# First layer of a graph network: seven buffers for the equal-edge comparisons, and source numbers spread over the partitions by TensorE

## The chip, the cores and the metric

The kernel runs on one core of a Trainium2 chip. A core has five engines with a queue of instructions each: TensorE (PE; its weight loads are listed as PEld), VectorE (DVE), ScalarE (ACT), GpSimd (POOL) and SyncE (SP), which here only issues DMAs. They meet through semaphores. The metric is the device time of one execution in microseconds.

## The reference, cut to what matters

A network of four graph layers with residual and layer norm; 6250 nodes of 256 features, 100000 edges sorted by destination. The change touches the first layer's sum over edges and what is computed beside it:

```python
gathered = edge_val[:, None] * x[edge_col]                    # edge_row = src, edge_col = dst
support = jax.ops.segment_sum(gathered, edge_row, num_segments=N)
out = jax.nn.relu(jnp.concatenate([x, support], axis=1) @ W + b)
x = layernorm(x + out)
```

So each edge takes the row of `x` at its destination, times its weight, and adds it to the row of its source in `support`. Destinations are sorted, sources are not. The later layers sum by destination (attention, and two of normalised or plain sums).

## The kernel before

`scatter_by_source` (L1546) is the stage of the first layer. The edges stand in 784 tiles of 128 (`P`); a loop of 49 turns handles 16 tiles (`RING`) each, in two halves of 8 (`HALF`). Every engine runs its own written-out loop over the same turns; what orders them are the semaphores, there is no scheduler. In a tile:

- DVE makes two 128x128 matrices (L1823, L1825): `onehots`, which edge has which destination within a window of 128 nodes, and `same_source`, which edges of the tile have the same source, times their weights. For `same_source` it compares `source_row`, the tile's 128 source numbers along the free dimension, the same on all partitions, with `source_float`, the same numbers one per partition. There are four buffers of each (`BUFS`), so DVE can be four tiles ahead (`crossed`).
- PE multiplies them to `cross` (L1751), adds to the edge counts by destination (`counts_bank`, L1757), ACT copies `cross` to SBUF (L1709), PE multiplies it with the window of `x` (`rows_bank`, L1728), ACT copies the result to `rows` (L1686), and POOL adds the 128 rows to `support` in HBM with an indirect DMA (L1606). Equal sources of one tile all carry the full sum, so all but one of them must go to spare rows.
- That is what `index_half` (L1776) works out on DVE, eight tiles at once: it compares `source_row` with `source_float` again, masked by `earlier` (`scrap`, L1781), and puts the row numbers of the next half into `index` (L1795). It comes after the eight tiles of a half, and before DVE adds the half's counts to `histogram` (L1835). The read of a window's base into a register stands at each half's head.

`source_row` is loaded by SP (L1659), one broadcast DMA from HBM to 128 partitions per half (512 KB), in int32. SP waits before it until `same_source` of the half that stood there is done.

Beside it, in this first pass, the stage adds up values of equal edges. Seven times a turn (`NEAR`), before every second tile from tile 2 to tile 14, DVE compares `tail_row`, seven tiles of keys on all partitions, with `tail_key` (`compare`, L1807); the result goes into one of two buffers `same_edge`, and PE multiplies it with `near_values` into `totals` (`add_same`, L1739), matmuls with two columns, 15 a turn. Before it overwrites a buffer DVE waits until PE has used it (`same_used`). `tail_row` is loaded once a turn by SP (L1637), first in the turn's list, as soon as the seventh comparison of the turn before is done. SP's list of a turn is: `tail_row`, then for each half the window of `x`, zeros for `matrix`, `source_row`, zeros again.

A matmul of float32 operands is two instructions here, each with its weight load.

## Time and profile before

| | us |
|---|---|
| median of 3 runs | 7642.86 |
| lowest, highest | 7641.15, 7646.06 |
| the profiled execution, its own time | 7624.4 |
| its span in the profile | 7622.7 |
| the stage's turns in it | 114.8 to 1995.4 |

The profile is of one execution. A group of instructions is named by the engine, the line and the tiles, written<-read. "Busy" is time in which the engine executes, "idle before" the time in front of an instruction with what ended it in brackets. The granted clock is TensorE's: 1.0 is 2.4 GHz, 0.5 is 1.2 GHz. PE is busy for 80% of the whole span, POOL for 67%, DVE for 44%, ACT for 19%. A turn of the stage's loop shows in the timeline as the same pattern every 38 us or so.

### The profile page before, as it was taken

To read this page: it belongs to the slowest core of one execution; us is meant where nothing else is said; L and a number is where in the kernel's file an instruction comes from. 1 tells how busy PE (TensorE), PEld (TensorE's weight loads), DVE (VectorE), ACT (ScalarE), POOL (GpSimd) and SP (SyncE) were. 2 spreads that over 40 slices of the span, in tenths; PEclk is the share of its full clock that TensorE was granted. 3 is DMA by queue.
4 is the path that set the end of the run, shared out by engine and by line. 5 is a ranking of instruction groups with operands and counts; after the bars stand their busy time and mean duration, and the time that the engine had idled before them with its cause. 6 is when DMAs were issued, how large, how long until landed. Compare 5 with 4: busy or idle time off the path is not lost. (4 is left out here: it accounts for less than half of the span.)

```text
span 7622.7 us, 120614 instructions
## 1 busy us (share of the span) xinstructions
PE 6092.7 (80%) x30188; PEld 4294.4 (56%) x30188; DVE 3383.4 (44%) x13118; ACT 1434.8 (19%) x5010; POOL 5078.8 (67%) x4839
## 2 busy tenths in 40 slices
PE   3777777777673788886777777999799989998997
PEld 2445454444562565555666665666566656665655
DVE  3444444444353666664555553444333323333444
ACT  1222222222221122221222221111101000010001
POOL 3666666666674677775777775666577767776775
PEclk9777777777686999996555558999899999999998
DMA  7877777777532444442333337888599979988996
GB/s 261 192 176 146 153 156 155 155 156 155 114 105 82 112 116 117 116 117 73 82 80 82 83 83 236 287 283 286 190 318 312 309 256 319 308 265 297 305 308 214
DMA packets 752803, 1440.90 MB, mean 189 GB/s; under 512 B 155688, under 2 KB 483292, under 8 KB 749956
## 3 DMA queue, kind: packets, MB, share of 16 engines
q1 hardware_dynamic: 460276, 886.96, 34.2%
q0 software_dynamic: 289936, 523.75, 30.7%
q10 hardware_dynamic: 2304, 26.74, 0.8%
q8 instruction: 134, 2.20, 0.1%
q14 instruction: 153, 1.25, 0.1%
HBM read 1140.97 MB, written 295.98 MB: 189 GB/s over the span
## 5 line engine op out<-in xcount | busy, mean ns | idle before, releaser
L736 POOL DMA_INDIRECT rows<-gcn_rows,index x1632 | 1551.0, 950 | 658.0 <-issue 456.5
L1277 POOL DMA_INDIRECT rows<-gat_rows,index x1568 | 1500.3, 957 | 640.8 <-issue 463.7
L1606 POOL DMA_INDIRECT support<-rows,index x784 | 1211.9, 1546 | 691.9 <-ACT rows L1686 399.5
L832 PEld LDWEIGHTS bank<-onehots,rows 128*128 128x128 f32 x8704 | 1143.7, 193 | 607.9 <-issue 547.0
L832 PE MATMUL bank<-onehots,rows 128*128 128x128 f32 x8704 | 1181.3, 278 | 159.2 <-DMA rows<-gcn_rows,index 77.6
L1408 PE MATMUL bank<-onehots,rows 128*128 128x128 f32 (+1 forms) x4704 | 946.9, 338 | 328.5 <-DVE rows L1484 328.0
L1408 PEld LDWEIGHTS bank<-onehots,rows 128*128 128x128 f32 (+1 forms) x4704 | 720.6, 202 | 530.0 <-issue 323.0
L844 PE MATMUL dense_bank<-matrix,edge_space 128*128 128x512 f32 x1792 | 892.7, 619 | 0.0
L1751 PE MATMUL cross_bank<-same_source,onehots 128*128 128x128 f32 x1568 | 428.9, 363 | 569.8 <-DVE same_source L1825 569.8
L736 POOL DMA_INDIRECT rows<-norm,index x544 | 516.5, 949 | 286.3 <-issue 152.0
L1751 PEld LDWEIGHTS cross_bank<-same_source,onehots 128*128 128x128 f32 x1568 | 334.3, 243 | 661.1 <-issue 534.8
L844 PE MATMUL dense_bank<-alpha,edge_space 128*128 128x512 f32 x1344 | 670.3, 620 | 12.7 <-DVE acc L899 12.7
L1728 PE MATMUL rows_bank<-x_window,cross 128*128 128x256 f32 x1568 | 659.2, 514 | 0.0
L881 DVE TENSOR_SCALAR onehots<-iota,half_offset,edge_values 128x128 f32<-128x128 f32 x2176 | 589.3, 363 | 26.7 <-issue 8.1
L844 PEld LDWEIGHTS dense_bank<-matrix,edge_space 128*128 128x128 f32 x1792 | 310.7, 193 | 240.4 <-issue 239.1
L1781 DVE SCALAR_TENSOR_TENSOR scrap<-source_row,edge_space,earlier 128x128 f32<-128x128 int32 x792 | 224.6, 348 | 440.1 <-DMA source_row<-in_src_flat 440.1
L1728 PEld LDWEIGHTS rows_bank<-x_window,cross 128*128 128x128 f32 x1568 | 284.1, 227 | 220.6 <-issue 214.4
L1709 ACT COPY cross<-cross_bank 128x128 f32<-128x128 f32 x784 | 208.6, 266 | 967.9 <-PE counts_bank L1757 967.4
L1686 ACT COPY rows<-rows_bank 128x256 f32<-128x256 f32 x784 | 292.1, 373 | 401.6 <-PE rows_bank L1728 398.7
L1479 DVE TENSOR_SCALAR onehots<-iota,half_offset 128x128 f32<-128x128 f32 x1568 | 361.9, 302 | 8.8
L1757 PE MATMUL counts_bank<-onehots,values 128*3 128x128 f32 x1568 | 359.9, 319 | 0.0
L844 PEld LDWEIGHTS dense_bank<-alpha,edge_space 128*128 128x128 f32 x1344 | 234.1, 193 | 196.0 <-issue 194.5
(305 smaller groups left out, 7253.4 us busy)
## 6 DMA issues: line engine op xcount, KB each, us to landing
matrix<-matrix SPq DMA_DIRECT2D x448, 512.0 KB, 4.0
alpha<-matrix SPq DMA_DIRECT2D x336, 512.0 KB
matrix<-zeros SPq DMA_DIRECT2D x196, 512.0 KB, 8.0
edge_space<-gcn_rows SPq DMA_DIRECT2D x588, 128.0 KB, 5.2
dst_row<-in_dst_flat SPq DMA_DIRECT2D x100, 512.0 KB
source_row<-in_src_flat SPq DMA_DIRECT2D x99, 512.0 KB, 7.5
support<-zeros ACTq DMA_DIRECT2D x16, 1632.0 KB, 28.0
rows<-gcn_rows,index POOLq DMA_INDIRECT x1632, 5.2
```

The source lines that it names most:

```text
L736: nc.gpsimd.indirect_dma_start(rows[:, k, :], None, table, bass.IndirectOffsetOnAxis(ap=index[:, k:k + 1], axis=0),).then_inc(gathered[k], 16)
L832: done = nc.tensor.matmul(by_chunk(banks[h])[:, c, :], rows[:, k, c * P:(c + 1) * P], onehots[:, k, :], start=first and c == 0, stop=final ...
L844: done = nc.tensor.matmul(dense_banks[c][:, 0:GROUP], table_rows[:, n, c * P:(c + 1) * P], matrix[n].rearrange("p (n v) -> p n v", v=2)[:, ...
L881: made = nc.vector.tensor_scalar(onehots[:, k, :], g.iota[:], g.half_offset[:, tile], weights[:, 0, tile], ALU.is_equal, ALU.mult)
L1277: nc.gpsimd.indirect_dma_start(rows[:, k, :], None, table, bass.IndirectOffsetOnAxis(ap=index[:, k:k + 1], axis=0),).then_inc(gathered[k], 16)
L1408: done = nc.tensor.matmul(to, left, onehots[:, k, :], start=first and c == 0, stop=final and c == chunks - 1)
L1479: made = nc.vector.tensor_scalar(onehots[:, k, :], g.iota[:], g.half_offset[:, bass.ds(i * RING + k, 1)], None, ALU.is_equal)
L1606: nc.gpsimd.indirect_dma_start(support[k % COPIES], bass.IndirectOffsetOnAxis(ap=index[:, k // HALF, k % HALF:k % HALF + 1], axis=0), rows ...
L1686: nc.scalar.copy(rows[:, k % HALF, :], rows_bank[k % 2][:, 0:g.features]).then_inc(s.rows_ready, 1)
L1728: nc.tensor.matmul(rows_bank[k % 2][:, 0:g.features], cross[:, k % BUFS, :], x_window[:, k // HALF, :], start=True, stop=True).then_inc(s. ...
L1751: nc.tensor.matmul(cross_bank[k % 2][:, 0:P], onehots[:, b, :], same_source[:, b, :], start=True, stop=True)
L1757: nc.tensor.matmul(counts_bank[k // HALF][0:3, 0:P], values[:, k // HALF, k % HALF, :], onehots[:, b, :], start=(k % HALF == 0), stop=(k % ...
```

## The change

`same_edge` gets seven buffers, one for each comparison of a turn; DVE waits for the use of the same buffer in the turn before, not for the use two comparisons ago. ACT's `keep_totals` waits for the same use by a number that fits the new start value.

`source_row` is no longer loaded. ACT copies the eight columns of `source_float` of the next half to `source_columns`. PE takes each of these columns, repeated to 128, as the stationary operand and the identity matrix as the moving one, which gives the column's 128 numbers along the free dimension on all partitions, in float32. Four of them fill one PSUM bank, `row_bank`; ACT copies it to `source_row`. A half needs two such batches, issued after tiles 2 and 4 of the half before, and ACT's copies stand before those of tiles 3 and 5. `index_half` waits for the second copy (`row_ready`). To free a PSUM bank the two halves' counts share one.

```diff
-        source_row = sbuf("source_row", [P, 2, HALF, P], INT32)
+        source_row = sbuf("source_row", [P, 2, HALF, P])
+        source_columns = sbuf("source_columns", [P, HALF])
...
-            same_edge = sbuf("same_edge", [P, 2, 3 * P])
+            same_edge = sbuf("same_edge", [P, NEAR, 3 * P])
...
-        counts_bank = [psum(f"counts_bank{n}") for n in range(2)]
+        counts = psum("counts_bank")
+        counts_bank = [counts[:, h * P:(h + 1) * P] for h in range(2)]
+        row_bank = psum("row_bank")
...
-                        sync.wait_ge(s.matrices, i * RING + HALF * (h + 1))
-                        sync.dma_start(
-                            source_row[:, h, :, :].rearrange("p k e -> p (k e)"),
-                            g.source_flat[0:1, bass.ds((i * 2 + h) * (HALF * P), HALF * P)]
-                            .to_broadcast([P, HALF * P])).then_inc(row_loaded[h], 16)
...
+                def copy_columns(half):
+
+                    if not isinstance(half, int):
+                        act.wait_ge(s.row_turned, half * 2)
+                    act.sem_inc(s.issued, 1)
+                    nc.scalar.copy(source_columns[:], g.source_float[:, bass.ds(half * HALF, HALF)]
+                                   ).then_inc(s.columns_ready, 1)
+
+                def copy_row(half, h, batch):
+
+                    act.wait_ge(s.row_turned, half * 2 + (batch + 1))
+                    if not isinstance(half, int) and batch == 0:
+                        act.wait_ge(s.matrices, half * HALF + (RING - HALF))
+                    act.sem_inc(s.issued, 1)
+                    nc.scalar.copy(source_row[:, h, batch * BATCH:(batch + 1) * BATCH, :].rearrange("p k e -> p (k e)"),
+                                   row_bank[:]).then_inc(s.row_ready, 1)
...
+                        if k % HALF == 1:
+                            copy_columns(i * 2 + (k // HALF + 1))
+                        if k % HALF == 3:
+                            copy_row(i * 2 + (k // HALF + 1), 1 - k // HALF, 0)
+                        if k % HALF == 5:
+                            copy_row(i * 2 + (k // HALF + 1), 1 - k // HALF, 1)
...
+                def source_rows(half, batch):
+
+                    if batch == 0:
+                        pe.wait_ge(s.columns_ready, half + 1)
+                    if batch or not isinstance(half, int):
+                        pe.wait_ge(s.row_ready, half * 2 + batch)
+                    for n in range(BATCH):
+                        column = source_columns[:, batch * BATCH + n:batch * BATCH + n + 1].to_broadcast([P, P])
+                        done = nc.tensor.matmul(row_bank[:, n * P:(n + 1) * P], column, g.identity[:], start=True,
+                                                stop=True)
+                    done.then_inc(s.row_turned, 1)
...
+                        if k % HALF in (2, 4):
+                            source_rows(i * 2 + (k // HALF + 1), k % HALF // 2 - 1)
...
-                    dve.wait_ge(row_loaded[h], i * 16 + 16 * (ahead + 1))
+                    dve.wait_ge(s.row_ready, i * 4 + (2 * (2 * ahead + h) + 2))
...
-                    dve.wait_ge(s.same_used, i * NEAR + max(2, r + 1))
+                    dve.wait_ge(s.same_used, i * NEAR + (r + 1))
...
-                    nc.vector.tensor_scalar(same_edge[:, r % 2, 0:(high - low + 1) * P], tail_row[:, low * P:(high + 1) * P],
+                    nc.vector.tensor_scalar(same_edge[:, r, 0:(high - low + 1) * P], tail_row[:, low * P:(high + 1) * P],
```

On PE, tile 2 of a turn before the change (the names are tiles, written<-moving operand, stationary operand; REGISTER_ALU works out a semaphore's value):

```order
L1751 MATMUL cross_bank_418<-same_source,onehots 128x128
L1757 MATMUL counts_bank_422<-onehots,values 3x128
L1725 REGISTER_ALU
L1728 MATMUL rows_bank_421<-x_window,cross 128x256
L1734 ISA
L1739 MATMUL totals<-near_values,same_edge 128x2
L1748 REGISTER_ALU
L1751 MATMUL cross_bank_419<-same_source,onehots 128x128
```

And after it:

```order
L1784 MATMUL cross_bank_419<-same_source,onehots 128x128
L1790 MATMUL counts_bank<-onehots,values 3x128
L1744 REGISTER_ALU
L1747 MATMUL rows_bank_422<-x_window,cross 128x256
L1753 ISA
L1758 MATMUL totals<-near_values,same_edge 128x2
L1765 REGISTER_ALU
L1767 REGISTER_ALU
L1770 MATMUL row_bank<-identity,source_columns 128x128 x4
L1781 REGISTER_ALU
L1784 MATMUL cross_bank_420<-same_source,onehots 128x128
```

The four source matmuls stand between the tile's `totals` and the next tile's `cross`; tile 4 and the second half have the same.

On ACT, between the copies of tiles 2 and 3 before the change (`rows` of tile 1, then `cross` of tile 3):

```order
L1683 REGISTER_ALU
L1686 COPY rows<-rows_bank_421 128x256
L1708 REGISTER_ALU
L1709 COPY cross<-cross_bank_419 128x128
```

And after it:

```order
L1676 REGISTER_ALU
L1679 COPY rows<-rows_bank_422 128x256
L1703 REGISTER_ALU
L1705 REGISTER_ALU
L1707 COPY source_row<-row_bank 128x512
L1727 REGISTER_ALU
L1728 COPY cross<-cross_bank_420 128x128
```

The copy of the source rows, with its wait, now stands ahead of the copy of `cross`.

On SP, the start of a turn's list before the change:

```order
L1637 DMA tail_row<-key_row 128x896
L1651 TENSOR_LOAD half_base
L1651 ISA x2
L1655 ISA
L1655 DMA x_window<-in_x 128x256
L1645 DMA matrix<-zeros 128x1024
L1659 DMA source_row<-in_src_flat 128x1024
L1645 DMA matrix<-zeros 128x1024
```

And after it:

```order
L1640 DMA tail_row<-key_row 128x896
L1654 TENSOR_LOAD half_base
L1654 ISA x2
L1658 ISA
L1658 DMA x_window<-in_x 128x256
L1648 DMA matrix<-zeros 128x1024 x2
```

The source load and the wait before it are gone, the two loads of zeros stand together.

## Rows read from the trace of the kernel before

**Rows 1.** Who waited for whom, 104 to 2004 us: total us, times, longest.
```profile
PE cross_bank L1751 <- DVE same_source L1825: 569.8, 98, 82.2
...
DVE scrap L1781 <- DMA source_row<-in_src_flat: 440.1, 49, 12.9
...
DVE same_edge L1807 <- PE totals L1739: 349.9, 147, 3.9
...
POOL support L1606 <- issue: 193.8, 516, 4.9
```

**Rows 2.** The instructions that write `cross_bank`: min/median/max ns, first and last start.
```profile
L1751 PE MATMUL cross_bank<-same_source,onehots x1568: 272/356/582, 114.8 to 1995.4; 128*128 128x128 f32 x196
```

**Rows 3.** Busy time by stretch: length, PE, PEld, DVE, ACT, POOL, granted clock, DMA.
```profile
500.00:1900.00 1400.00, 1033.89 (x4581) 685.93 (x4580) 577.09 (x2798) 390.87 (x1308) 895.49 (x580) 0.75 0.73 154
...
1020.00:1029.50 9.50, 9.50 (x32) 6.34 (x33) 2.93 (x11) 2.25 (x8) 6.16 (x4) 0.50 0.65 96
...
1035.00:1042.00 7.00, 0.00 (x0) 0.00 (x0) 3.48 (x22) 0.78 (x4) 4.60 (x3) 0.64 1.10 286
...
1042.00:1047.00 5.00, 4.82 (x15) 2.69 (x16) 2.76 (x13) 1.04 (x4) 0.02 (x1) 0.50 0.59 137
```

**Rows 4.** Timeline of DVE at a turn's middle and end: start, length, what, [idle before].
```profile
1016.18 0.28 DVE L1835 TENSOR_TENSOR histogram<-histogram,counts_bank 3x128 f32 x1 [2.13 <-PE counts_bank L1757]
...
1026.30 0.29 DVE L1807 TENSOR_SCALAR same_edge<-tail_row,tail_key 128x128 f32<-128x128 f32 x1 [3.89 <-PE totals L1739]
...
1036.00 0.35 DVE L1781 SCALAR_TENSOR_TENSOR scrap<-source_row,edge_space,earlier 128x128 f32<-128x128 int32 x1 [8.13 <-DMA source_row<-in_src_flat]
...
1039.07 0.17 DVE L1795 TENSOR_TENSOR index<-moved,edge_space 128x8 int32<-128x8 f32 x1 [0.48 <-DMA support<-rows,index]
...
1039.30 0.28 DVE L1835 TENSOR_TENSOR histogram<-histogram,counts_bank 3x128 f32 x1
```

**Rows 5.** Timeline of SP at the same turn's end.
```profile
1026.75 0.33 SPq L1637 DMA_DIRECT2D tail_row<-key_row  x1
...
1029.08 0.33 SPq L1659 DMA_DIRECT2D source_row<-in_src_flat  x1
```

**Rows 6.** Timeline of PE in the same turn and at its end.
```profile
1010.65 0.38 PE L1751 MATMUL cross_bank<-same_source,onehots 128*128 128x128 f32 x2
...
1011.82 0.50 PE L1739 MATMUL totals<-near_values,same_edge 128*128 128x2 f32 x4
...
1018.32 0.49 PE L1751 MATMUL cross_bank<-same_source,onehots 128*128 128x128 f32 x2 [1.74 <-DVE same_source L1825]
...
1021.13 0.59 PE L1757 MATMUL counts_bank<-onehots,values 128*3 128x128 f32 x2
...
1023.23 0.59 PE L1757 MATMUL counts_bank<-onehots,values 128*3 128x128 f32 x2
...
1042.18 0.79 PE L1751 MATMUL cross_bank<-same_source,onehots 128*128 128x128 f32 x2 [7.23 <-DVE same_source L1825]
```

**Rows 7.** PE in a later stage, timeline and granted clock of a stretch.
```profile
4635.96 2.04 PE L832 MATMUL bank<-onehots,rows 128*128 128x128 f32 x8 [19.25 <-DMA rows<-norm,index]
...
4637.80 3.62 PE L844 MATMUL dense_bank<-alpha,edge_space 128*128 128x512 f32 x4
...
4644.48 1.05 PE L832 MATMUL bank<-onehots,rows 128*128 128x128 f32 x8
...
4645.36 1.97 PE L844 MATMUL dense_bank<-alpha,edge_space 128*128 128x512 f32 x4
...
4636.00:4637.00 1.00, 1.00 (x5) 1.00 (x6) 1.00 (x6) 0.00 (x0) 0.69 (x2) 0.50 1.05 385
```

**Rows 8.** Groups of the page: count, busy us, mean ns, idle before by releaser.
```profile
L1606 POOL DMA_INDIRECT support<-rows,index x784 | 1211.9, 1546 | 691.9 <-ACT rows L1686 399.5
...
L1686 ACT COPY rows<-rows_bank 128x256 f32<-128x256 f32 x784 | 292.1, 373 | 401.6 <-PE rows_bank L1728 398.7
```

More of the change, by code:

```diff
@@ L1576, in scatter_by_source @@
         rows_bank = [psum(f"rows_bank{n}") for n in range(2)]
-        counts_bank = [psum(f"counts_bank{n}") for n in range(2)]
+        counts = psum("counts_bank")
+        counts_bank = [counts[:, h * P:(h + 1) * P] for h in range(2)]
+        row_bank = psum("row_bank")
         names = [f"scattered{k}" for k in range(HALF)]
-        with phase(nc, "kept", "x_loaded0", "x_loaded1", "row_loaded0", "row_loaded1", "own", "index_ready",
+        with phase(nc, "kept", "x_loaded0", "x_loaded1", "columns_ready", "row_turned", "row_ready", "own", "index_ready",
                    "issued", "matrices", "crossed", "cross_copied", "multiplied", "rows_ready", "counted",
@@ L1582, in scatter_by_source @@
             scattered = s[-HALF:]
-            x_loaded, row_loaded = [s.x_loaded0, s.x_loaded1], [s.row_loaded0, s.row_loaded1]
+            x_loaded = [s.x_loaded0, s.x_loaded1]
             @block.gpsimd
@@ L1671, in _ @@
                     sync.wait_ge(s.kept, 16 * len(later))
-                sync.wait_ge(s.matrices, g.tiles + HALF)
-                sync.dma_start(source_row[:, 0, :, :].rearrange("p k e -> p (k e)"),
-                               g.source_flat[0:1, 0:HALF * P].to_broadcast([P, HALF * P])
-                               ).then_inc(row_loaded[0], 16)
             @block.scalar
@@ L1693, in keep_totals @@
                 def keep_totals(i):
-                    act.wait_ge(s.same_used, i * NEAR + (NEAR + 2))
+                    act.wait_ge(s.same_used, i * NEAR + 2 * NEAR)
                     act.sem_inc(s.issued, 1)
@@ L1698, in keep_totals @@
                                    ).then_inc(s.near_ready, 1)
+                def copy_columns(half):
[11 more added lines that the diff above has]
+                                   row_bank[:]).then_inc(s.row_ready, 1)
                 if first_pass:
                     copy_near(0)
+                copy_columns(0)
+                for batch in range(2):
+                    copy_row(0, 0, batch)
                 with act.Fori(0, g.tiles // RING) as i:
                     for k in range(RING):
+                        if k % HALF == 1:
[4 more added lines that the diff above has]
+                            copy_row(i * 2 + (k // HALF + 1), 1 - k // HALF, 1)
                         if k % HALF == 0:
@@ L1738, in add_same @@
                     for w in range(low, high + 1):
-                        done = nc.tensor.matmul(totals[:, w - 1, :], same_edge[:, r % 2, (w - low) * P:(w - low + 1) * P],
+                        done = nc.tensor.matmul(totals[:, w - 1, :], same_edge[:, r, (w - low) * P:(w - low + 1) * P],
                                                 near_values[:, r, :], start=r == 0, stop=r == NEAR - 1)
                     done.then_inc(s.same_used, 1)
+                def source_rows(half, batch):
[8 more added lines that the diff above has]
+                    done.then_inc(s.row_turned, 1)
                 if first_pass:
-                    pe.sem_inc(s.same_used, 2)
+                    pe.sem_inc(s.same_used, NEAR)
+                for batch in range(2):
+                    source_rows(0, batch)
                 with pe.Fori(0, g.tiles // RING) as i:
```

## The prediction

> **What bounds the kernel now.** I read the list of who waited for whom first, for the first layer's stage. TensorE (PE) waits 98 times for `same_source` of VectorE (DVE), twice in each of the 49 turns; without the one long wait of 82.2 us at the start that is 487.6 us, or 9.95 us a turn. DVE waits 49 times, 440.1 us, for the DMA of `source_row`, and 147 times, 349.9 us, for PE's `totals` [rows 1]. The turns fill the time between the first and last `cross` matmul, 114.8 to 1995.4 us, so one turn takes 38.4 us [rows 2]. Inside the stage the granted clock is 0.75 on average, so PE stands at its lower level (1.2 GHz) for half of a turn, 19.2 us [rows 3].
>
> The timeline shows how a turn ends. DVE gets to its last comparison of equal edges, `same_edge` for r = 6, at 1026.30, after 3.89 us of waiting for `totals`, since two buffers are all it has. Only then may SyncE (SP) start `tail_row`, and the `source_row` load of the next turn's first half stands behind that in its queue: it starts at 1029.08 and lands for DVE's `scrap` at 1036.00, where DVE sat idle for 8.13 us. Comparisons, `index` and `histogram` follow, and PE gets its next `same_source` at 1042.18, after 7.23 us of idleness [rows 4 to 6]. So the late broadcast sets the turn, not its bandwidth. GpSimd (POOL) is no bound: 16 scatters of 1.55 us with 0.38 us between them (193.8 us / 516) are 30.8 us of 38.4, and most of its idle time is for ACT's `rows` [rows 1, 8].
>
> **Part by part, for one turn.** I split the turn into PE's work at full clock, its pauses, and what the low clock adds.
>
> A tile (cross, counts, rows) takes 1.17 us at full clock (1010.65 to 1011.82) and 2.10 us at the lower level (1021.13 to 1023.23) [rows 6]. So of each busy microsecond at the low level 1 - 1.17/2.10 = 0.44 is loss. Of the 7.0 us from 1035 to 1042, at 0.64 in the mean, 5.0 us were low while PE was idle [rows 3]; for the average pause at a turn's end of 8.2 us (9.95 less the 1.74 in the middle [rows 6]) I take 6.0. Low and busy are then 19.2 - 6.0 = 13.2 us, a loss of 5.8. Full-clock work is 38.4 - 9.95 - 5.8 = 22.6 us.
>
> *The pause at the turn's end.* With source rows out of PE and ACT, DVE needs no DMA there, and what is late next is the count of the half's last tile: `histogram` must come before the next half's matrices. In the middle of a turn this already is so, and it costs 1.74 us [rows 6]. There the way from `histogram` to PE's next matmul is 2.14 us (1016.18 to 1018.32), at the end it is 2.88 (1039.30 to 1042.18), for the register loads at the loop's head [rows 4, 6]; PE meanwhile has one more rows matmul to do (half a tile by its columns, 0.5). The end pause becomes 1.74 + 0.74 - 0.5 = 2.0 us, I take 2.1. That removes 6.1 us.
>
> *The source matmuls.* 16 a turn, four in a row, at tiles 2 and 4 of each half. Each is float32, 128x128 by 128x128, so two instructions. The nearest rows are runs of eight such instructions: 0.88 us at full clock (4644.48 to 4645.36), 1.84 us at the lower (4635.96 to 4637.80, granted clock 0.50) [rows 7]. Four runs are 3.5 us, and with 0.1 for each wait on a semaphore 4.0 us. From above, if each costs a quarter of a tile (which has four times 128 columns to move, `rows` counting twice), it is 16 x 0.29 + 0.4 = 5.1. They lie on PE's path, nothing hides them. None of the rows has a stationary operand that is one column repeated; I take it to cost what another does. A bound below nothing has no reason here.
>
> *ACT.* Four copies of 128x512 a turn and two of 128x8. A 128x256 copy is 0.37 us [rows 8], so 0.6 (at most 0.75) each: 2.6 us. ACT waits in order, so a copy that waits for `row_turned` holds back the copy of the next `cross`; but the four matmuls end before PE does the next cross and counts (0.6 us), which cover it. Nothing.
>
> *DVE's new wait.* `index_half` now waits for the second copy of source rows. After tile 3 is counted PE has half a tile, tile 4, a few `totals`, and two waits' worth of source matmuls (one run) to do, 3.1 us; copy 0.6; from the first `scrap` to `histogram` 3.30 (1036.00 to 1039.30) [rows 4]: 7.0 us. PE counts tile 7 after 3.1 + 1.2 + 1.2 + 0.5 + 0.6 = 6.6 us. At full clock DVE is later than before by 0.2 to 0.4, at the lower clock not at all. I put 0.2 a turn; bounds 0 and 2 (one per half).
>
> *Seven buffers.* DVE no longer waits for `totals` (7.1 us a turn), but it is then held by `crossed`, four tiles ahead of PE. Their use is that the last comparison, and so `tail_row` behind it, comes earlier: tile 9 is counted at 1021.7 (1021.13 and half a microsecond), so r = 6 could be done at 1022.5 in place of 1026.30, 3.8 us earlier [rows 4, 6]. By themselves they would thus take most of the pause away already. With the broadcast gone they only guard `tail_row` (448 KB by its size, against 512 KB of `source_row`, which took 6.9 us, 1029.08 to 1036.00 [rows 4, 5]): between comparison 6 and comparison 0 of the next turn PE does at least five tiles, a pause and two source runs, about 10 us.
>
> *DMA.* SP loses two loads and their waits per turn, 1 MB that landed in SBUF. Nobody waits for the others; nothing.
>
> *The low clock.* Now 13.2 us busy in it. In the turn shown it is there again at 1020, 1.7 us after PE resumes from the middle pause, and lasts at least the 9.5 us to 1029.5 while PE is wholly busy; after the end pause it lasts about 5 us more (1042 to 1047 at 0.50) [rows 3]. So a pause of 1.74 us is enough to lose the clock, and I expect two falls a turn as before. How it comes back: with the denser work of rows 7 it was back within 5.3 us of 19 us of idleness (4635.96 low, the run at 4644.48 full). The source matmuls are work of that density, and `totals`, with two columns each, are the opposite. I take 5 us per pause, 10 in all, a loss of 4.4. Bounds: 5 and 20.
>
> **Sum.** Work 22.6 + 4.0, pauses 2.1 + 1.7 + 0.2, low clock 4.4: 35.0 us a turn, 3.4 less than 38.4. Over 49 turns 167 us, and some 3 us since the first half needs no load (of 12.9 us that DVE waits for it [rows 1], the tail and x loads keep most). The profiled execution, 7624.4 us with a span of 7622.7, would become about 7454. It lies 18.5 us under the median of 7642.86; I take the same difference for the median: 7473 us. What comes after the stage begins when it ends, and its work is the same.
>
> **The rivals.** Each as 30.6 + 0.44 x L, L being low-clock busy time; 17.7 us of L would give all back.
>
> 1. *The clock pays for it (slower).* Place: the 10 us after each of the two pauses. If each costs what the middle one costs now, 10 us, then L = 20 and the turn is 39.4 us: +49 us, 7690. It decides from L = 17.7. For it: more work at low clock lasts longer, and the trace has that 10 us stretch with PE wholly busy. Against: rows 7. The Trainium skill ("TensorE: Matmul & The Clock Gate", Part 4, PE-mode transpose) says that transposes through the array do not count as activity for the clock gate. A matmul against the identity does a transpose's work; if that held for these ordinary matmuls too, this rival would be the likeliest and the sum 7690, else 7473. No row before the change settles it. Chance 0.12.
>
> 2. *The clock stays up.* The end pause is short enough to lose nothing: L = 5, 32.8 us a turn, 7366. Against it: the middle pause is shorter and loses it. Chance 0.08.
>
> 3. *A new wait eats it.* DVE's wait for `row_ready` costs 1 us per half and a source matmul costs 0.29: 35.0 + 1.8 + 1.1 = 37.9, 7616; either alone, 7525 to 7565. For it: the margin is 0.4 us. Against it: at low clock there is none. Chance 0.17 for over 7560.
>
> 4. *The broadcast isn't what ends the pause*, since x, tail or a scatter is late just behind it. `index` waits for landed scatters, and `tail_row` still starts late. A pause of 4 us in place of 2.1 gives 36.9 us a turn, 7566. For it: DMA is the slowest releaser here. Against it: five tiles lie between. Counted in 3.
>
> **How the numbers follow.** Forecast, 7390 to 7560: 0.63; rival 1 0.12, rival 2 0.08, rivals 3 and 4 0.17 together. Of rival 3 0.02 and of rival 1 0.01 lie within 0.2% of 7643 (15 us, about what a measurement of this kernel can tell from no change). Faster 0.63 + 0.08 + 0.15 = 0.86, same 0.03, slower 0.11. The range leaves out rival 1 and half of rival 2: 7390 to 7620.
>
> **What the profile after would show.** The stage ends near 1830 us; PE idle before `cross` some 4 us a turn, not 9.95; no wait of DVE for `totals` or for a source load; `row_bank` runs of 0.9 us at full clock; the mean granted clock in the stage over 0.8. A mean clock of 0.7 or less would speak for rival 1; runs of 1.2 us or a `scrap` that starts after the last count for rival 3. The forecast is wrong if PE's pauses stay long for another load, or if L is over 15 us.

## The result, and the profile after

The changed kernel takes 7559.15 us (median of 4 runs, 7555.93 to 7571.13), the kernel before 7642.0 (4 runs, 7631.09 to 7646.06). The ratio is 0.9903 with an interval of 0.989 to 0.9916: 83 us or 0.97% faster. A second series gave 0.9913 (0.9891 to 0.9935). The forecast was 7473 us, 170 us faster. So the direction held, and half the gain is missing.

The profiled executions have spans of 7554.4 and 7622.7 us, 68.3 apart. Where they differ is read from the instructions that write `cross_bank` after the change (min/median/max ns, first and last start):

```profile
L1784 PE MATMUL cross_bank<-same_source,onehots x1568: 272/275/583, 105.8 to 1934.0; 128*128 128x128 f32 x196
```

The new tile `row_bank`, in the same view:

```profile
L1770 PE MATMUL row_bank<-identity,source_columns x1584: 275/275/579, 90.4 to 1931.2; 128*128 128x128 f32 x198
L1707 ACT COPY source_row<-row_bank x198: 586/586/587, 92.6 to 1931.6; 128x512 f32<-128x512 f32 x198
```

Against 114.8 to 1995.4 before [rows 2] the stage starts 9.0 us earlier and its 49 turns are 52.4 us shorter, 1828.2 in place of 1880.6: 37.3 us a turn, not 38.4. That is 61.4 of the 68.3 us. The other 7 us lie in later stages, whose work is the same.

Who waited for whom, 104 to 2004 us (total us, times, longest):

```profile
DVE onehots L1858 <- PE counts_bank L1790: 546.4, 245, 4.5
...
DVE scrap L1816 <- ACT source_row L1707: 349.3, 98, 3.9
ACT source_row L1707 <- PE row_bank L1770: 283.7, 196, 2.8
...
PE cross_bank L1784 <- DVE same_source L1860: 207.1, 98, 10.5
...
DVE index L1830 <- DMA support<-rows,index: 43.8, 89, 0.5
```

These answer to [rows 1]. PE's 569.8 us of waiting for `same_source` are 207.1 now; without the one wait of 10.5 us at the start that is 4.0 us a turn, 9.95 before. DVE's waits for `totals` (349.9) and for the source load (440.1) are gone. Thus 5.9 us of idleness a turn went, but the turn is only 1.1 us shorter. The rest became work, and more of it under a lower clock. By stretch (length; busy time of PE, PEld, DVE, ACT, POOL; granted clock; DMA share and GB/s):

```profile
500.00:1900.00 1400.00, 1248.76 (x5893) 896.76 (x5891) 588.40 (x2872) 490.00 (x1570) 921.56 (x596) 0.77 0.69 132
1037.70:1041.10 3.40, 3.40 (x12) 2.08 (x12) 2.63 (x11) 1.24 (x5) 2.29 (x3) 0.56 1.09 278
1041.20:1051.30 10.10, 9.33 (x59) 6.91 (x58) 3.43 (x21) 4.65 (x14) 7.99 (x6) 0.99 0.60 67
1051.50:1065.00 13.50, 12.61 (x44) 9.35 (x45) 5.15 (x20) 2.86 (x9) 6.85 (x5) 0.51 0.64 154
1065.10:1075.20 10.10, 7.92 (x46) 5.43 (x46) 4.49 (x27) 4.32 (x15) 7.27 (x5) 0.99 0.65 116
```

The mean clock of the stage is 0.77, against 0.75 [rows 3]. PE is busy 89% of the time, not 74% (1248.76 and 1033.89 of 1400). One turn is four stretches: 3.4 us at the lower level (1.2 GHz, 0.50) after the pause at the turn's end, 10.2 us full, 13.7 us low from within the pause in the middle on, 10.2 us full. (The windows shown start up to 0.4 us beside the steps.) The steps of the granted clock in the trace lie at 1038.08, 1041.49, 1051.73 and 1065.39. PE's timeline over the same turn:

```profile
1036.74 0.48 PE L1784 MATMUL cross_bank<-same_source,onehots 128*128 128x128 f32 x2 [2.16 <-DVE same_source L1860]
...
1045.23 1.14 PE L1770 MATMUL row_bank<-identity,source_columns 128*128 128x128 f32 x8
1046.21 0.39 PE L1784 MATMUL cross_bank<-same_source,onehots 128*128 128x128 f32 x2
...
1052.39 0.79 PE L1784 MATMUL cross_bank<-same_source,onehots 128*128 128x128 f32 x2 [1.87 <-DVE same_source L1860]
...
1060.12 1.28 PE L1758 MATMUL totals<-near_values,same_edge 128*128 128x2 f32 x6
1061.26 2.05 PE L1770 MATMUL row_bank<-identity,source_columns 128*128 128x128 f32 x8
1063.10 0.64 PE L1784 MATMUL cross_bank<-same_source,onehots 128*128 128x128 f32 x2
...
1074.27 0.48 PE L1784 MATMUL cross_bank<-same_source,onehots 128*128 128x128 f32 x2 [2.18 <-DVE same_source L1860]
...
1089.91 0.79 PE L1784 MATMUL cross_bank<-same_source,onehots 128*128 128x128 f32 x2 [1.86 <-DVE same_source L1860]
```

Two things are to be seen. A run of four source matmuls takes 0.98 us at full clock (1045.23 to 1046.21) and 1.84 us at the lower (1061.26 to 1063.10); of the four runs of a settled turn three are at full clock and only this one is at the lower. And the next turn repeats this one: 1036.74 to 1074.27 and 1052.39 to 1089.91 are 37.5 us each, with the same pauses. By the distance between `histogram` instructions three early turns take 33.1, 34.8 and 37.7 us, and every one after them 37.4 to 37.7 us with halves of 21.6 and 15.9. Turns before the change vary between about 36 and 41 us.

### The profile page after: what moved, and what is told of

It is laid out like the page before. It is cut to its first block and busy times, and to the rows that moved or that the text cites. A ratio compares the mean times of both kernels' runs of the same rounds, so it can differ in the third digit from the quotient of the medians.

```text
span 7554.4 us, 124892 instructions
## 1 busy us (share of the span) xinstructions
PE 6340.0 (84%) x31772; PEld 4550.9 (60%) x31772; DVE 3376.6 (45%) x13118; ACT 1550.6 (21%) x5307; POOL 5078.6 (67%) x4839
## 3 DMA queue, kind: packets, MB, share of 16 engines
q0 software_dynamic: 289936, 523.75, 31.1%
## 5 line engine op out<-in xcount | busy, mean ns | idle before, releaser
L1747 PE MATMUL rows_bank<-x_window,cross 128*128 128x256 f32 x1568 | 683.8, 530 | 0.0
L1784 PE MATMUL cross_bank<-same_source,onehots 128*128 128x128 f32 x1568 | 399.3, 343 | 207.1 <-DVE same_source L1860 207.1
L1858 DVE TENSOR_SCALAR onehots<-iota,half_offset 128x128 f32<-128x128 f32 x784 | 248.8, 318 | 605.5 <-PE counts_bank L1790 546.4
L1816 DVE SCALAR_TENSOR_TENSOR scrap<-source_row,edge_space,earlier 128x128 f32<-128x128 f32 x792 | 224.4, 350 | 353.3 <-ACT source_row L1707 349.3
L1479 DVE TENSOR_SCALAR onehots<-iota,half_offset 128x128 f32<-128x128 f32 x1568 | 361.1, 301 | 8.2
```

Of the source, the lines that this page charges most:

```text
L1479: made = nc.vector.tensor_scalar(onehots[:, k, :], g.iota[:], g.half_offset[:, bass.ds(i * RING + k, 1)], None, ALU.is_equal)
L1747: nc.tensor.matmul(rows_bank[k % 2][:, 0:g.features], cross[:, k % BUFS, :], x_window[:, k // HALF, :], start=True, stop=True).then_inc(s. ...
L1784: nc.tensor.matmul(cross_bank[k % 2][:, 0:P], onehots[:, b, :], same_source[:, b, :], start=True, stop=True)
```

## The experiments

**How each turn is counted.** The forecast's own sum is used for every kernel: 22.6 us of full-clock work, the added matmuls, PE's idleness, and 0.44 for each busy microsecond at the lower level (L). Idleness and L are added up from PE's instructions and the steps of the granted clock, over the stage without its first and last turns; "turn" is the first to the last `cross` matmul over 49. The 22.6 was solved from the kernel before, so its row agrees by construction. In the others a turn is PE's busy and idle time in any case; what the agreement within 0.6 us tests is that the work without the matmuls stays 22.6 us and that 0.44 and the matmuls' price are right. The ratio is to the kernel before in the same series. PE's idleness is nearly all before `cross`, except in e4, e7, e8, e10 and e11, where 0.5 to 2.3 us of it stand elsewhere.

| kernel | ratio [interval] | added matmuls | idle | L | sum | turn, us |
|---|---|---|---|---|---|---|
| before | 1 | 0 | 10.1 | 13.5 | 38.6 | 38.4 |
| changed | 0.9903 [0.989, 0.9916] | 3.9 | 4.0 | 16.1 | 37.6 | 37.3 |
| e5, changed again | 0.9913 [0.9891, 0.9935] | 3.9 | 4.0 | 16.4 | 37.7 | 37.5 |
| e2, source matmuls only | 0.9933 [0.9911, 0.9956] | 3.9 | 4.0 | 16.4 | 37.7 | 37.4 |
| e1, seven buffers only | 0.9787 [0.975, 0.9824] | 0 | 6.2 | 14.2 | 35.0 | 34.9 |
| e12, the same again | 0.9741 [0.9722, 0.976] | 0 | 6.5 | 13.6 | 35.1 | 34.9 |
| e3, fill in the middle pause | 0.9618 [0.9575, 0.9662] | 3.9 + 1.6 | 2.7 | 3.5 | 32.3 | 31.8 |
| e9, fill in the end pause | 0.9703 [0.9676, 0.9731] | 3.9 + 1.6 | 2.5 | 8.7 | 34.4 | 34.1 |
| e6, fill before tile 14 | 0.9745 [0.9724, 0.9766] | 3.9 + 1.6 | 3.2 | 8.5 | 35.0 | 34.7 |
| e4, source matmuls in the pauses | 0.9597 [0.9562, 0.9633] | 3.9 | 3.4 | 4.2 | 31.7 | 31.1 |
| e11, the same again | 0.952 [0.9495, 0.9545] | 3.9 | 3.2 | 4.5 | 31.7 | 31.1 |
| e7, load before tail | 0.9693 [0.9671, 0.9715] | 0 | 5.5 | 13.1 | 33.9 | 33.8 |
| e10, e7 with seven buffers | 0.971 [0.9685, 0.9736] | 0 | 5.3 | 13.8 | 34.0 | 33.9 |
| e8, e7 with fill in both pauses | 0.9704 [0.9687, 0.9722] | 3.2 | 4.5 | 8.6 | 34.1 | 34.0 |

e1 to e4 ran in a series in which the other stages are slower (before takes 8994.7 us there; from the last `cross` matmul to the end e1 takes 7019 us and e12, the same kernel, 5618). This stage is as long as elsewhere: 34.9 us a turn in both e1 and e12, 31.1 in both e4 and e11. The ratios of that series are therefore nearer to 1 for the same saving, and the turn is what compares.

### e1 and e12: seven buffers alone

```diff
-            same_edge = sbuf("same_edge", [P, 2, 3 * P])
+            same_edge = sbuf("same_edge", [P, NEAR, 3 * P])
...
-                    pe.sem_inc(s.same_used, 2)
+                    pe.sem_inc(s.same_used, NEAR)
...
-                    dve.wait_ge(s.same_used, i * NEAR + max(2, r + 1))
+                    dve.wait_ge(s.same_used, i * NEAR + (r + 1))
```

ACT's wait in `keep_totals` changes along with them. The source load stays a DMA.

> The kernel before with seven buffers alone; the broadcast DMA of the source numbers stays. The clock theory (of the changed kernel's turn of 37.5 us, 16.3 us are busy work at the low clock, where 10 were forecast, and most of them follow the middle pause; pauses and matmul costs are as forecast): the last comparison of a turn ends 3.8 us earlier, the pause at the turn's end goes from some 8.4 to 4 to 5 us; with as much low clock as before a turn of 34.6 us (7455 us in all), with 16 us of low clock 36 us (7525). The rival theory (the added source matmuls, 4 us a turn on TensorE's path, take back what the shorter pause gives, and the clock only goes along): 34.6 us a turn, 7455, faster than the changed kernel by 100 us.

Measured: 8823.98 against 8994.7 us; turn 34.9 us. Since this is faster than the whole change, it was run again where the other stages run as in the first series.

> The kernel before with seven buffers alone, once more: its first run was on a chip on which all other stages were slower. By the balance it keeps its turn of 34.9 us on any chip, 3.5 us less than before, so the kernel before less 170 to 190 us, and faster than the whole change by some 100 us. If the first ratio (0.979) came from that chip's slower DMA, it comes out near the changed kernel's 0.990.

Measured: 7444.65 against 7636.9 us, 192 us less, interval 0.9722 to 0.976. Waits of e12 over its stage:

```profile
PE cross_bank L1751 <- DVE same_source L1825: 392.6, 98, 82.1
DVE scrap L1781 <- DMA source_row<-in_src_flat: 266.1, 55, 12.9
```

And a stretch of it (columns as above):

```profile
500.00:1600.00 1100.00, 896.92 (x3959) 596.40 (x3960) 500.91 (x2422) 337.21 (x1129) 780.87 (x504) 0.77 0.82 171
```

PE's wait for `same_source` falls from 569.8 to 392.6 us and DVE's for the source load from 440.1 to 266.1 [rows 1]: about 3.6 us a turn, all of it kept, since L hardly moves (13.5 and 13.6). The buffers alone give more than twice what the change gives.

### e2: the source matmuls alone

The changed kernel with the buffers put back (and with them PE's start value and ACT's wait):

```diff
-            same_edge = sbuf("same_edge", [P, NEAR, 3 * P])
+            same_edge = sbuf("same_edge", [P, 2, 3 * P])
...
-                    dve.wait_ge(s.same_used, i * NEAR + (r + 1))
+                    dve.wait_ge(s.same_used, i * NEAR + max(2, r + 1))
```

> The changed kernel with two buffers of same_edge in place of seven. Both theories: VectorE waits for totals again, but between the last comparison and the next tail_row lies time enough, so within 0.2% of the changed kernel's 7559 us. If the buffers carry a part of the gain it is slower by up to 3.8 us a turn, 7745.

Measured: 8940.8 us, ratio 0.9933; turn 37.4 us. Its waits:

```profile
DVE same_edge L1842 <- PE totals L1758: 385.6, 142, 3.9
PE cross_bank L1784 <- DVE same_source L1860: 206.6, 98, 10.4
```

And PE's timeline where it waited:

```profile
1005.53 0.48 PE L1784 MATMUL cross_bank<-same_source,onehots 128*128 128x128 f32 x2 [2.16 <-DVE same_source L1860]
...
1021.16 0.80 PE L1784 MATMUL cross_bank<-same_source,onehots 128*128 128x128 f32 x2 [1.85 <-DVE same_source L1860]
...
1043.01 0.48 PE L1784 MATMUL cross_bank<-same_source,onehots 128*128 128x128 f32 x2 [2.17 <-DVE same_source L1860]
```

DVE again waits 385.6 us for `totals`, and PE waits no longer than in the changed kernel, with the same two pauses and the same 37.5 us between turns. Once the source rows come from PE, the buffers hide nothing that anyone waits for. The parts overlap: each removes the same late load, the buffers for nothing, the matmuls for 3.9 us of PE's time and 2.9 us more at the lower clock.

### e3: seven unread matmuls in the middle pause

The changed kernel with matmuls that nobody reads, just ahead of PE's wait for tile 8:

```diff
+        idle_bank = psum("idle_bank")
...
+                        if k == HALF:
+                            for _ in range(7):
+                                nc.tensor.matmul(idle_bank[:, 0:P], g.identity[:], g.identity[:], start=True, stop=True)
                         pe.wait_ge(s.matrices, i * RING + (RING + k + 1))
```

> The changed kernel plus seven matmuls of the identity by itself, whose result nobody reads, in the pause in the middle of each turn (before TensorE's wait for tile 8's matrices): 1.6 us of added work in a pause of 1.9 us. Clock theory: the pause no longer costs the clock, the low stretch of 13.7 us that follows it in every turn goes, 0.44 x 13 = 5.7 us less a turn: 31.8 to 33 us a turn, 7280 to 7340 us in all. Rival theory: 37.5 us a turn or more, 7559 to 7600, whatever the clock does.

Measured: 8671.7 us, ratio 0.9618; turn 31.8 us. PE's timeline at e3's two pauses:

```profile
1013.13 0.48 PE L1788 MATMUL cross_bank<-same_source,onehots 128*128 128x128 f32 x2 [2.21 <-DVE same_source L1864]
...
1026.70 1.72 PE L1784 MATMUL idle_bank<-identity 128*128 128x128 f32 x14
1028.72 0.49 PE L1788 MATMUL cross_bank<-same_source,onehots 128*128 128x128 f32 x2 [0.30 <-DVE same_source L1864]
```

And its stretch:

```profile
500.00:1600.00 1100.00, 1013.87 (x6010) 749.19 (x6011) 565.43 (x2687) 453.60 (x1467) 869.66 (x561) 0.95 0.82 157
```

1.6 us of work without use shorten the turn by 5.5 us (269 us in all against e2 of the same series, whose turns are those of the changed kernel). The middle pause shrinks from 1.87 to 0.30 us, the mean clock goes from 0.77 to 0.95, and L from 16.1 to 3.5. This shows that the lower clock holds back the missing time, and how much it is: 0.44 x 12.6 = 5.5 us a turn.

The pause at the end, 2.2 us, is as long as before, and yet 12 of the 47 turns counted have no low clock at all. A stretch of 57.9 us at full clock with such a pause in it:

```profile
1048.30:1106.20 57.90, 53.04 (x334) 39.92 (x333) 29.33 (x141) 25.25 (x81) 46.38 (x30) 1.00 0.81 147
...
1076.51 0.48 PE L1788 MATMUL cross_bank<-same_source,onehots 128*128 128x128 f32 x2 [2.16 <-DVE same_source L1864]
```

So a pause of this length goes with a fall in every settled turn of the changed kernel and does not bring one by itself.

### e6 and e9: the same matmuls elsewhere

Is it the pause that costs the clock, or is there simply too little matmul work? e6 has the same seven at `if k == HALF + 6:`, where PE doesn't pause; e9 at `if k == 0:`, in the pause at the turn's end.

> The changed kernel plus the same seven matmuls of the identity once a turn, not in a pause but before tile 14, where TensorE has no pause of note. Clock theory: the work is the same as in the kernel that fills the middle pause, but the pause still costs the clock, so 0 to 1.6 us more a turn: 37.5 to 39.1 us a turn, the changed kernel plus 0 to 80 us. If the seven matmuls helped by their number alone, wherever they stand, it would be some 270 us faster than the changed kernel, as the kernel with the middle pause filled was.

> The changed kernel plus the seven unread matmuls of the identity in the pause at the turn's end alone (ahead of the wait for tile 0). In the changed kernel the low stretch after that pause is 3.4 us, the one after the middle pause 13.7 us. Clock theory: the short one goes, 1.5 us less a turn, and the long one stays: 36 us a turn, the kernel before less 140 to 170 us, so far less than with the middle pause filled (less 323 us). If any added dense work helps alike, less 300 us or more.

Measured: e6 7435.16 us against 7566.85 for the changed kernel (e5) in that series, 132 less, where none or a loss was expected. e9: 7402.63 against 7623.3 for before, 221 less where 140 to 170 was expected; turn 34.1 where 36 was. PE's timeline of e6, with the fill and both pauses:

```profile
1005.49 1.72 PE L1784 MATMUL idle_bank<-identity 128*128 128x128 f32 x14
...
1011.38 0.48 PE L1788 MATMUL cross_bank<-same_source,onehots 128*128 128x128 f32 x2 [1.18 <-DVE same_source L1864]
...
1025.73 0.49 PE L1788 MATMUL cross_bank<-same_source,onehots 128*128 128x128 f32 x2 [2.10 <-DVE same_source L1864]
```

Its stretch:

```profile
500.00:1600.00 1100.00, 997.80 (x5444) 733.07 (x5444) 499.29 (x2441) 411.01 (x1325) 788.55 (x508) 0.87 0.74 142
```

The fill and the end pause of e9:

```profile
1026.09 1.73 PE L1784 MATMUL idle_bank<-identity 128*128 128x128 f32 x14
1028.42 0.48 PE L1788 MATMUL cross_bank<-same_source,onehots 128*128 128x128 f32 x2 [0.61 <-DVE same_source L1864]
```

Its stretch:

```profile
500.00:1600.00 1100.00, 1021.35 (x5543) 756.45 (x5542) 502.82 (x2474) 420.10 (x1352) 803.25 (x518) 0.87 0.76 146
```

In both, one low stretch a turn is left (of 6.8 to 13.7 us in e6, of 6.8 or 10.2 in e9, once 3.4); it follows the middle pause, and L is 8.5 and 8.7. The theory "a filled pause saves what stood behind that pause" is too narrow: e9 fills the pause that has 3.4 us of low clock behind it, and the long stretch behind the other pause shrinks. e6 fills no pause; the one that follows is shorter (1.18, not 2.16 us): PE gets there later while DVE's matrices come when they came, so the matmuls may act in part as a fill of that pause. What stands: matmuls at any of three places shorten the turn by 2.6 to 5.5 us, the middle pause being the best of them.

### e4 and e11: the source matmuls in the pauses

If the pauses are there anyway, the work that the change adds can stand in them: both batches ahead of the wait of tiles 0 and 8, into two PSUM banks, with the column copies moved up.

```diff
-        row_bank = psum("row_bank")
+        row_bank = [psum(f"row_bank{n}") for n in range(2)]
...
-                        if k % HALF == 1:
-                            copy_columns(i * 2 + (k // HALF + 1))
-                        if k % HALF == 3:
+                        if k % HALF == 6:
+                            copy_columns(i * 2 + (k // HALF + 2))
+                        if k % HALF == 0:
                             copy_row(i * 2 + (k // HALF + 1), 1 - k // HALF, 0)
-                        if k % HALF == 5:
                             copy_row(i * 2 + (k // HALF + 1), 1 - k // HALF, 1)
...
+                        if k % HALF == 0:
+                            for batch in range(2):
+                                source_rows(i * 2 + (k // HALF + 1), batch)
                         pe.wait_ge(s.matrices, i * RING + (RING + k + 1))
...
-                        if k % HALF in (2, 4):
-                            source_rows(i * 2 + (k // HALF + 1), k % HALF // 2 - 1)
```

> The changed kernel with both batches of source matmuls (eight in a row, two PSUM banks) moved to the head of each half, before TensorE waits for the next half's matrices, so into its two pauses of about 2 us; the copies on ScalarE move along, and the columns are copied half a turn earlier. Clock theory: 3.6 us leave the path and both pauses are filled, so the clock falls less often: 26.8 us + 0.44 x 5 = 29 us, then GpSimd's 30.8 us of scatters is the bound: 31 us a turn, 7240 to 7300 in all. Rival theory: 37.5 - 3.6 = 33.9 us a turn, 7380.

> The kernel with the source matmuls in the pauses once more, beside the others of this call on one chip: a turn of 31.1 us as in its first run, the kernel before less 340 to 370 us, and faster than the reordered kernels by over 60 us.

Measured: e4 8635.94 us, ratio 0.9597; e11 **7259.11 us** (7254.89 to 7261.07) against 7623.3, ratio 0.952, interval 0.9495 to 0.9545. That is 364 us below the kernel before and 144 below e10 of the same series. Waits of e11 over its stage:

```profile
DVE index L1831 <- DMA support<-rows,index: 298.0, 86, 7.6
POOL support L1609 <- DMA support<-rows,index: 185.1, 396, 5.3
```

PE's timeline at the end of a pause with source matmuls in it:

```profile
1013.08 2.05 PE L1770 MATMUL row_bank<-identity,source_columns 128*128 128x128 f32 x16
1018.67 0.64 PE L1787 MATMUL cross_bank<-same_source,onehots 128*128 128x128 f32 x2 [3.54 <-DVE same_source L1861]
```

And its stretch:

```profile
500.00:1600.00 1100.00, 990.94 (x5629) 717.10 (x5629) 565.57 (x2734) 466.56 (x1493) 888.06 (x573) 0.93 0.82 160
```

The pauses did not both fill: the middle one is gone in 43 of 48 turns, the one at the end stands in 41 and is 2.3 us in the mean, behind the source matmuls. The same sixteen matmuls a turn cost 3.9 us as before, but the clock is 0.93 and L 4.5, nearly all of it behind the end pause. The turn is 31.1 us, and now DVE's `index` and POOL wait for scatters to land, 298.0 and 185.1 us. 16 scatters with what lies between them are 30.8 us by [rows 1, 8], so little more is to be had in front of POOL.

### e7, e8 and e10: the late load without any matmul

The load was late because SP issues `tail_row` first and that waits for the last comparison. So the kernel before, with `tail(i)` after the loads of the first half:

```diff
                 def loads(i):
-                    tail(i)
                     for h in range(2):
+                        if h == 1:
+                            tail(i)
```

> The kernel before (two buffers, broadcast DMA, no source matmuls) with one change in SyncE's list: tail_row is issued after the loads of a turn's first half and not ahead of them, so that the late load of source_row no longer stands behind the wait for the last comparison. Clock theory: the source numbers are there in time, the pauses are 4 us a turn as in the changed kernel, without its 4 us of source matmuls: 22.6 + 4.0 + 0.44 x (13 to 16) = 32.3 to 33.7 us a turn, the kernel before less 230 to 300 us. If the DMA itself were the bound (its bandwidth, or the scatters beside it), the turn would stay over 36 us.

> The same with seven unread matmuls of the identity at the head of each half, ahead of TensorE's wait for matrices. Clock theory: both pauses are filled, the clock stays up most of the time: 22.6 + 4.0 + 0.44 x 2 = 27.5 us, under GpSimd's 30.8 us of scatters, which then is the bound: 31 us a turn, the kernel before less 360 us or more. If the filled pauses give nothing, it is as the kernel with the reordered load alone, or up to 80 us slower.

> The kernel before with the reordered load and seven buffers, no source matmuls. What binds there by the balance 22.6 + pauses + 0.44 x low clock: VectorE no longer waits for totals (336.8 us in the reordered kernel), which were not on TensorE's path; so pauses of 4 to 5.5 us a turn and 33 to 34 us a turn, as the reordered kernel alone, the kernel before less 230 to 280 us.

Measured: e7 7395.44 us against 7633.26, ratio 0.9693 (238 us less, within the 230 to 300 expected) with a turn of 33.8 and 5.5 us of idleness where 4.0 were expected. e8, with e3's seven matmuls in both pauses (`if k % HALF == 0:`), 7403.71, ratio 0.9704, far from the 360 us expected. e10, e7 with seven buffers, 7403.68 against 7623.3, 220 less where 230 to 280 was expected; its ratio of 0.971 can't be told from e7's by the intervals. Waits of e7 over its stage:

```profile
DVE index L1796 <- DMA support<-rows,index: 280.6, 96, 9.1
...
DVE scrap L1782 <- DMA source_row<-in_src_flat: 63.7, 48, 2.9
```

And of e8:

```profile
DVE index L1800 <- DMA support<-rows,index: 374.2, 96, 12.1
ACT rows L1688 <- DMA support<-rows,index: 307.0, 206, 9.1
POOL support L1607 <- DMA support<-rows,index: 256.9, 371, 8.2
```

One line moved in SP's list takes DVE's wait for the load from 440.1 to 63.7 us [rows 1] and gives nearly three times the change's gain. The buffers add nothing to it: both cure the same thing. What is late next is the landing of the scatters, beside the 1 MB of source loads that still run. In e8 L falls from 13.1 to 8.6, worth 2.0 us, and idleness by 1.0, but 3.2 us of matmuls came in. `index` waits for scatters 94 us more than in e7, and ACT's `rows`, 116.4 us in e7, waits 307.0; PE then waits for ACT too, 107.8 us in place of 25.7:

```profile
PE rows_bank L1730 <- ACT cross L1711: 107.8, 99, 7.2
```

By these waits the matmuls bought clock that the scatters ate. In e11 the loads are gone, DVE waits 298.0 us and ACT's `rows` 111.5 in a turn that is 2.9 us shorter. This would be the one use of doing without the DMA; no run varies the DMA load by itself, so that step is argued from the two kernels' waits and not shown.

### e5: the changed kernel again

> The changed kernel itself, beside the kernels of this call on one chip. Both theories: its stage of the first layer takes the same 1828 us from first to last cross matmul as in the profile of the changed kernel (turn 37.3 us), and it is 60 to 90 us faster than the kernel before, whatever the other stages take on this chip.

Measured: 7566.85 against 7633.26 us, ratio 0.9913; stage 105.4 to 1943.0 us, turns of 37.5 us. The result came again.

## Why the prediction was half right

*The late load ends the turn.* Right: e7 changes only its place in the queue and gets 238 us.

*The pauses, 4.0 us a turn in place of 9.95.* Right: 207.1 us less 10.5 over 49 turns is 4.0; single pauses are 2.16 at the end (predicted 2.1) and 1.87 in the middle (1.74 and a part of the 0.2 of delay).

*The source matmuls, 4.0 us a turn.* Right. Runs of 0.98 and 1.84 us stand where the nearest rows had 0.88 and 1.84 [rows 7]; four at full clock are 3.9. The higher bound, a quarter of a tile each, was not needed, and a stationary operand of one repeated column costs what another does.

*ACT.* Right: 0.586 us a copy, 0.6 taken.

*DVE's new wait.* Right in size. In the middle of a turn `histogram` now starts straight behind `index`, where before it had waited 2.13 us for PE's count [rows 4]:

```profile
1050.30 0.17 DVE L1830 TENSOR_TENSOR index<-moved,edge_space 128x8 int32<-128x8 f32 x1 [0.50 <-DMA support<-rows,index]
1050.53 0.28 DVE L1870 TENSOR_TENSOR histogram<-histogram,counts_bank 3x128 f32 x1
```

PE's middle pause grew by 0.13 us against the one turn that the prediction read, and by 0.35 in the mean of the stage (1.54 to 1.89). So rival 3 had its mechanism, at a tenth to a third of its price. Rival 4, another load late, did not come: `index` waits at most 0.5 us for scatters.

*The start.* 9.0 us earlier, 3 predicted: tail and x loads held less of the first wait than assumed.

*Seven buffers.* The text said that the last comparison would come 3.8 us earlier and that this alone "would thus take most of the pause away already". It took 3.6 us, under half of the 8.2 at the turn's end. But the sum was never made for this part alone: 38.4 - 3.8 = 34.6 us a turn was there to be read, below the 35.0 forecast for the whole. e12 measured 34.9. The gain was credited to the pair, and the matmuls' own share, by the forecast's own terms, was below nothing. Measured, the matmuls make e12's 7444.65 into about 7559, some 110 us slower (in different series, whose times for before differ by 0.1%).

*The low clock.* This is the step that failed: "I take 5 us per pause, 10 in all, a loss of 4.4." Measured are 3.4 and 13.7 us, less about 0.7 in which PE was idle: L = 16.4 in each such turn, a loss of 7.2 us. That is 2.8 us a turn more than taken, 137 us over 49 turns, and covers the whole 113 us by which the stage missed its 35.0 us a turn (37.3 measured; the sum from measured parts gives 37.6). The term was bounded by 5 and 20, and the value was taken from the neighbour that suited: rows 7 say how fast the clock comes back in dense work after 19 us of idleness (by the clock's own step 5.5 us, where the text has 5.3). The prediction's own 13.2 us for the kernel before already said more: kept as it was, it gives 36.4 us a turn. No row gave a reason for it to fall to 10. The row of this stage, 9.5 us low with PE wholly busy after the middle pause [rows 3], said about 10 for that pause alone. It was called rival 1 and given 0.12, and what came is that rival stopped short of its break-even of 17.7. With 5 for the end and 10 for the middle the sum would have been 15 x 0.44 = 6.6 and 37.2 us a turn. That this comes so near is partly luck: the row was one turn with a long stretch, and in the mean of the stage before, 7.5 us of L stand behind the middle pause and 6.0 behind the end. After the change it is 12.8 and 3.3: the whole growth is behind the middle pause.

*The range and the signs.* The measured 7559 lies in the stated range of 7390 to 7620 and just within the forecast's 7390 to 7560, but with L at 16.1 and not 10, so the range did not hold it for its reason. The sign that it named for being wrong came: L is over 15 us. The mean clock is 0.77, not over 0.8, and the stage ends at 1934 us, not near 1830. Rival 2, the clock staying up, did not come.

*Rival 1's other ground.* The source matmuls do not fail to hold the clock. e3 puts seven plain matmuls against the identity into a pause and the mean clock goes from 0.77 to 0.95; e11 does it with the source matmuls themselves, 0.93. The Trainium skill ("TensorE: Matmul & The Clock Gate", Part 4) says of transposes in the array's transpose mode that they do not count as busy time in the same way; if that were read as a rule for an ordinary float32 matmul against the identity, these runs would speak against it. No run here has a transpose of that mode, so what it says of those stays open. What mattered was where the matmuls stand: behind tiles 2 and 4 of each half, three of the four runs come when the clock is up and one in the middle of the low stretch; ahead of tiles 0 and 8 the clock falls less often, L 4.5 in place of 16.1.

*What stays open.* Why the turns of the changed kernel (and of e2 and e5) settle into identical ones of 37.5 us, with one low stretch of 13.7 us in each, across two groups of six `totals`. Both small changes of a turn (e6, e9) ended this pattern, and in e3 a pause of 2.2 us often brings no fall, so part of the 16.4 us may belong to it and not to the pauses' lengths. A run that shifts the turn's length a little and leaves PE's work as it is could tell; none was made.

## What to carry to other kernels

When two edits attack one wait, make the sum for each alone and then for the pair: the second often pays its full price for a wait that the first removed, and one line's place in a DMA queue may do what both do. Where TensorE sits at its lower clock for half a stage, price added matmuls by where they stand: with sixteen of them in the pauses the turn took 31.1 us here, with the same sixteen between tiles 37.3 us. For the low clock take the rows of the same stage, and of two neighbours the one that speaks against the change when the break-even (17.7) lies near the bound.

## What the runs showed of the hardware

- Seven unread 128x128 float32 matmuls, 1.6 us, made a turn of 37.3 us one of 31.8 us, with the granted clock at 0.95 in place of 0.77 (e3).
- Pauses of TensorE of 1.87 and 2.16 us were accompanied or followed by the fall to the lower level in every settled turn of the changed kernel; with the first of them it stayed for 13.7 us, in which PE was idle for under 1 us. In e3 a pause of 2.16 us stood in a stretch of 57.9 us at full clock: the length of a pause did not decide it alone.
- The changed loop settled into one pattern together with the clock's changes: turns of 37.5 us, equal to 0.2 us, over more than 40 turns, each with one low stretch of 3.4 and one of 13.7 us, where the kernel before has turns of about 36 to 41. Which of the two follows the other no run tells.
- A float32 matmul with a stationary operand that is one column repeated over 128 costs as any other: 0.98 us for eight instructions at full clock, 1.84 at the lower.
